# Indirect gathers with an add in the transfer become plain copies added by the vector engine, in a two-layer mixture-of-experts kernel

## The reference, cut to what matters

```python
x = L0_attn_a_x                                  # 8 x 512 x 128, f32
x = x + attn_a(layernorm(x), ...)                # causal, 16 heads, RoPE
x = x + ffn(layernorm(x), sel, keys, values)     # layer 0 of the experts
x = x + attn_b(layernorm(x), WQ, WK, WV)         # band of 64, one head
x = x + ffn(layernorm(x), sel, keys, values)     # layer 1, same weights

def ffn(x, expert_sel, keys, values):            # 64 experts of size 128
    sel = sigmoid(x @ expert_sel.T)
    sel_val, sel_idx = top_k(sel, 4)
    gates = zeros.at[token, sel_idx].set(sel_val)
    return sum_e (relu(x @ keys[e]) * gates[:, e]) @ values[e]
```

## Time and profile before

| what | value |
|---|---|
| three runs | 1194.97, 1205.8 and 1199.96 us, median 1199.96 us |
| span of the profiled execution | 1216.6 us from first to last instruction |
| what lies around the span | no time is given for it |
| POOL busy | 876.4 us, 72% of the span |
| PE busy | 818.3 us, 67% |
| DVE busy | 728.4 us, 60% |
| ACT busy | 560.2 us, 46% |

### The profile page before, as it was taken

One profiled execution on the slowest core, in us unless ns is written; L12 is line 12 of the kernel. 1 busy time (PEld: TensorE's weight loads), 2 busy tenths in 40 slices (PEclk: granted clock), 3 DMA queues, 4 the chain that ended last, 5 costly groups with the idle time before them and its releaser, 6 DMA issues.

```text
span 1216.6 us, 22596 instructions
## 1 busy us (share of the span) xinstructions
PE 818.3 (67%) x7290; PEld 601.3 (49%) x7290; DVE 728.4 (60%) x2057; ACT 560.2 (46%) x1505; POOL 876.4 (72%) x934
## 2 busy tenths in 40 slices
PE   1899978888688766697898665454458874991000
PEld 0444444443344325697898644343357774991000
DVE  3787988888878424764667846566256772661111
ACT  1177666676566743564565413333126552661000
POOL 6345667879767675887888878878727578887776
PEclk9789999999999986898999866567679897996555
DMA  6556544533272332599898412212325564994222
GB/s 182 171 181 210 191 159 172 171 99 105 75 232 58 96 95 76 144 264 215 176 215 177 81 44 42 39 46 37 100 72 162 149 183 127 263 273 106 69 63 63
DMA packets 226258, 163.80 MB, mean 135 GB/s; under 512 B 15968, under 2 KB 213600, under 8 KB 226144
## 3 DMA queue, kind: packets, MB, share of 16 engines
q1 hardware_dynamic: 183968, 110.43, 31.7%
q0 software_dynamic: 36096, 33.59, 13.8%
q10 hardware_dynamic: 6080, 18.35, 4.1%
HBM read 78.94 MB, written 83.36 MB: 133 GB/s over the span
## 4 chain that ended last, share of the span: by engine, by line
PE 37%; POOL 23%; DVE 15%; issue 14%; ACT 6%; another core or an unknown queue 3%; DMA 3%; ACTq 0%; POOLq 0%; DVEq 0%; SPq 0%
POOL x_res L1743 7%; PE ps L771 6%; PE ps L780 5%; PE ps L672 5%; POOL sorted_rows L1727 4%; POOL v_aug L1745 3%; PE ps L631 3%; PE ps L760 3%; POOL x_scaled L1745 2%; ACT arena L978 2%; DMA x_res<-result_rows,dest 2%; DVE row_max L1211 2%; PE ps L689 2%; POOL arena L1776 1%
## 5 line engine op out<-in xcount | busy, mean ns | idle before, releaser
L1743 POOL DMA_INDIRECT x_res<-result_rows,dest x176 | 274.1, 1557 | 60.6 <-issue 48.8
L978 ACT ACTIVATE arena<-ps 128x512 f32<-128x512 f32 x320 | 182.8, 599 | 79.9 <-PE ps L604 75.1
L1727 POOL DMA_INDIRECT sorted_rows<-v_aug,dest x144 | 139.7, 970 | 83.7 <-issue 33.8
L1410 DVE COPY arena<-ps 128x512 f32<-128x512 f32 x128 | 88.2, 689 | 132.0 <-PE ps L760 71.7
L771 PE MATMUL ps<-arena 128*128 128x128 f32 x1024 | 147.2, 290 | 23.0 <-DVE arena L1410 11.5
L631 PE MATMUL ps<-arena 64*128 64x128 bf16 (+3 forms) x576 | 130.2, 305 | 28.9 <-DMA arena<-k_parts 15.1
L771 PEld LDWEIGHTS ps<-arena 128*128 128x128 f32 x1024 | 134.4, 205 | 26.9 <-issue 13.9
L1211 DVE TENSOR_REDUCE row_max<-ps 128x1 f32<-128x512 f32 (+1 forms) x192 | 127.0, 682 | 33.6 <-PE ps L651 31.9
L967 ACT COPY arena<-ps 128x512 f32<-128x512 f32 x128 | 75.0, 586 | 145.6 <-PE ps L780 117.0
L780 PE MATMUL ps<-arena 128*128 x1024 | 140.1, 281 | 0.9 <-ACT arena L967 0.9
L1727 POOL DMA_INDIRECT sorted_rows<-x_scaled,dest x112 | 111.5, 995 | 35.9 <-issue 24.6
(11 more groups left out here) (207 smaller groups left out, 1649.5 us busy)
## 6 DMA issues: line engine op xcount, KB each, us to landing
arena<-sorted_rows SPq DMA_DIRECT2D x128, 256.0 KB
result_rows<-arena SPq DMA_DIRECT2D x128, 256.0 KB
sorted_rows<-arena ACTq DMA_DIRECT2D x16, 1024.0 KB, 4.6
arena<-q_parts SPq DMA_DIRECT2D x16, 512.0 KB, 4.0
arena<-k_parts SPq DMA_DIRECT2D x16, 512.0 KB, 5.0
q_parts<-parts SPq DMA_DIRECT2D x52, 128.0 KB, 2.8
k_parts<-parts SPq DMA_DIRECT2D x38, 128.0 KB, 3.0
x_res<-result_rows,dest POOLq DMA_INDIRECT x176
```

What stands on the lines that cost most here:

```text
L978: nc.scalar.activation(prob[:, grp % 2, pr % 2, PROB_AT[u]:PROB_AT[u] + T], ps[:, v % 2, :], ACT.Exp, scale=SCALE_A).then_inc(exp_done, 1)
L1410: nc.vector.tensor_copy(xtt[:, n % 2, :], ps[:, e_bank(0, layer, half, n), :]).then_inc(t1_done, 1)
L1727: g.indirect_dma_start(sorted_d[b // HALF][:, :], bass.IndirectOffsetOnAxis(dest[:, 16 * b + n:16 * b + n + 1], 0), scaled_rows(layer, b)[ ...
L1743: g.indirect_dma_start(x[:, TT * b + t, :], None, rows, index, compute_op=ALU.add).then_inc(lane, 16)
```

## The change

Three things. **(a)** All 16 batches are gathered by plain copies. Each choice c of a batch goes into a slice of 128x512 of its own (`gathered_slice`), in buffers that are free at that time: in layer 0 two sets in turn (`x_scaled`; and one of `w_attn`, `parts`, `max_t`, `arena`), in layer 1 seven sets. A copy into a slice waits until the add of the slice's last user is done (`slice_freed`). **(b)** DVE adds one slice at a time: layer 0's batch 0 before iteration -1, batch b + 2 at four places of iteration b; layer 1's slices behind every second expert step of the last half from step 8 on, the others after the last step. The gathers of batches 5 to 7 of layer 0 move one iteration ahead in POOL's row. **(c)** The 74 clearings `rest` are gone.

```diff
-PLAIN = tuple((1, b) for b in range(3, B))
-PACED_FROM = 5
+ADD_FROM, ADD_EACH = 8, 2
...
+def gathers_ahead(it):
+    return {-1: (2,), 0: (3,), 1: (4, 5)}.get(it, ())
+def gathers_behind(it):
+    return {2: (6,), 3: (7,)}.get(it, ())
+def added_count(layer, b, c):
+    return TOPK * (B * layer + b) + c + 1
...
-        mt = sb("max_t", [32, 2, T], BF16)
+        max_room = sb("max_t", [P, 2, T], BF16)
+        mt = max_room[0:32, :, :]
...
+        spare = [w[:, 0:T], parts[:, 2].rearrange("p n t -> p (n t)").bitcast(F32),
+                 max_room[:, :, :].rearrange("p n t -> p (n t)").bitcast(F32), arena[:, 9504:9504 + T]]
+        heads = [ytf[:, i, :] for i in range(8)]
+        ropes = [qt[0], qt[1], kt[0], kt[1]]
+        first_homes = (four_slices(xs_a), spare)
+        second_homes = (four_slices(xs_a), four_slices(xs_b[:, 0]), four_slices(xs_b[:, 1]), spare, heads[0:4], heads[4:8], ropes)
...
+        def slice_freed(layer, b, c):
+            if layer == 0:
+                return added_count(0, b - 2, c) if b >= 2 else 0
+            before = {0: (0, B - 2), 3: (0, B - 1), 7: (1, 0)}
+            return added_count(*before[b], c) if b in before else 0
...
-            def add_rows(layer, b):
+            def add_rows(layer, b, c):
-                xb = x[:, TT * b:TT * b + TT, :]
-                for c in range(TOPK):
-                    for lane in landed:
-                        dve.wait_ge(lane, landed_count("gather", layer, b) - 16 * (TOPK - 1 - c))
-                    if c:
-                        dve.wait_ge(added, TOPK * PLAIN.index((layer, b)) + c)
-                    nc.vector.tensor_tensor(xb, xb, gathered_rows(layer, b)[:, TT * c:TT * c + TT, :], ALU.add).then_inc(added, 1)
+                xb = x[:, TT * b:TT * b + TT, :].rearrange("p t n -> p (t n)")
+                for lane in landed:
+                    dve.wait_ge(lane, landed_count("gather", layer, b) - 16 * (TOPK - 1 - c))
+                if c:
+                    dve.wait_ge(added, added_count(layer, b, c - 1))
+                nc.vector.tensor_tensor(xb, xb, gathered_slice(layer, b, c), ALU.add).then_inc(added, 1)
...
+                add_soon(b + 2, 0)
                 beside(b, 5)
...
             for s in range(STEPS):
                 expert_step(1, 1, s)
-            for b in range(B):
-                if (1, b) in PLAIN:
-                    add_rows(1, b)
+                if s >= ADD_FROM and (s - ADD_FROM) % ADD_EACH == 0:
+                    add_rows(1, *soon.pop(0))
+            for b, c in soon:
+                add_rows(1, b, c)
...
-                adding = (layer, b) not in PLAIN
-                if not adding and last_reader(layer, b):
-                    pool.wait_ge(added, last_reader(layer, b))
                 for c in range(TOPK):
+                    if slice_freed(layer, b, c):
+                        pool.wait_ge(added, slice_freed(layer, b, c))
                     for t in range(TT):
...
-                        if adding:
-                            g.indirect_dma_start(x[:, TT * b + t, :], None, rows, index, compute_op=ALU.add).then_inc(lane, 16)
-                        else:
-                            g.indirect_dma_start(gathered_rows(layer, b)[:, TT * c + t, :], None, rows, index).then_inc(lane, 16)
+                        g.indirect_dma_start(gathered_slice(layer, b, c)[:, P * t:P * t + P], None, rows,
+                                             bass.IndirectOffsetOnAxis(dest[:, at:at + 1], 0)).then_inc(lane, 16)
...
                     for n in range(TT * TOPK):
                         scatter(1, late, n)
-                        if late >= PACED_FROM:
-                            rest()
```

More of the change, by code:

```diff
@@ L156, in transfer_order @@
     for b in range(-1, LAST_IT_B + 1):
-        far, late = b + 3, b - 2
-        if b <= 1:
-            out.append(("gather", 0, far))
+        out += [("gather", 0, far) for far in gathers_ahead(b)]
+        late = b - 2
         if 0 <= late < B:
             out.append(("scatter", 1, late))
-        if 1 < b < B - 3:
-            out.append(("gather", 0, far))
+        out += [("gather", 0, far) for far in gathers_behind(b)]
     return out + [("gather", 1, b) for b in range(B)]
@@ L411, in scaled_rows, with four_slices, gathered_slice @@
             return xs_b[:, b % 2] if layer or b == B - 1 else xs_a
-        gather_buffers = (xs_a, xs_b[:, 0], xs_b[:, 1])
-        def gather_buffer(layer, b):
-            return b % 3 if layer else 0
-        def gathered_rows(layer, b):
-            return gather_buffers[gather_buffer(layer, b)]
-        def last_reader(layer, b):
-            mine = PLAIN.index((layer, b))
-            earlier = [n for n in range(mine) if gather_buffer(*PLAIN[n]) == gather_buffer(layer, b)]
-            return TOPK * (earlier[-1] + 1) if earlier else 0
+        def four_slices(rows):
+            return [rows[:, TT * c:TT * c + TT, :].rearrange("p t n -> p (t n)") for c in range(TOPK)]
+        spare = [w[:, 0:T], parts[:, 2].rearrange("p n t -> p (n t)").bitcast(F32),
[4 more added lines that the diff above has]
+        second_homes = (four_slices(xs_a), four_slices(xs_b[:, 0]), four_slices(xs_b[:, 1]), spare, heads[0:4], heads[4:8], ropes)
+        def gathered_slice(layer, b, c):
+            homes = second_homes if layer else first_homes
+            return homes[b % len(homes)][c]
+        def slice_freed(layer, b, c):
[3 more added lines that the diff above has]
+            return added_count(*before[b], c) if b in before else 0
         def scaled_in(it, k):
@@ L575, in _ @@
             for b in range(B):
-                if (1, b) not in PLAIN:
-                    for lane in landed:
-                        sp.wait_ge(lane, landed_count("gather", 1, b))
-                else:
-                    sp.wait_ge(added, TOPK * (PLAIN.index((1, b)) + 1))
+                sp.wait_ge(added, added_count(1, b, TOPK - 1))
                 sp.dma_start(out_d.rearrange("(t p) c -> p t c", p=P)[:, TT * b:TT * b + TT, :],
@@ L1585, in combined_stats @@
             def combined_stats(b):
-                if (0, b) in PLAIN:
-                    add_rows(0, b)
-                    dve.wait_ge(added, TOPK * (PLAIN.index((0, b)) + 1))
-                else:
-                    for lane in landed:
-                        dve.wait_ge(lane, landed_count("gather", 0, b))
+                dve.wait_ge(added, added_count(0, b, TOPK - 1))
                 finish(ln_stats(x[:, TT * b:TT * b + TT, :], st0, mv0, rs0, b, ln2))
@@ L1600, in _ @@
             dve.wait_ge(band_made, BANDS)
+            for c in range(TOPK):
+                add_rows(0, 0, c)
             for b in range(-1, LAST_IT_B + 1):
@@ L1705, in _ @@
             g.tensor_tensor(maskswap, maskswap, upper, ALU.add).then_inc(swapped, 1)
-            transfers, rests = count(), count(1)
-            def rest():
-                n = next(rests)
-                if n > 1:
-                    pool.wait_ge(rested, n - 1)
-                g.memset(w[:, :], 0.0).then_inc(rested, 1)
+            transfers = count()
             def next_lane():
@@ L1835, in _ @@
             gather(0, 0)
+            pool.wait_ge(parts_out, 192 * B)
+            for i in range(2):
+                pool.wait_ge(mrow_out[i], 16 * B)
             gather(0, 1)
             for b in range(-1, LAST_IT_B + 1):
-                far, late = b + 3, b - 2
-                if b <= 1:
+                late = b - 2
+                for far in gathers_ahead(b):
                     gather(0, far)
@@ L1846, in _ @@
                         scatter(1, late, n)
[L1847 to L1849 removed]
+                for far in gathers_behind(b):
                     gather(0, far)
```

15 lines of the change are left out of this document (8 added, 7 removed).

## The result

The changed kernel takes 1123.03 us (median of 4 runs, 1120.06 to 1127.7), the kernel before 1197.93 us beside it (1194.97 to 1205.8): ratio 0.9384, 95% interval 0.9352 to 0.9416, so 75 us (6.2%) faster. Forecast were 35 us and 1165, with a range down to 1135: the direction was right, and the size came out at twice the forecast and outside the range.

What follows compares the result with a forecast made beforehand. Bound by stretches: PE's expert steps, POOL from 696 to 892 us, PE and transfer engines from 1021, POOL alone at the end. Terms -24.3 - 11 + 4 - 7.7 + 4 = -35.0 us from 1199.96 gave 1165 us, range 1135 to 1212.

Steps and rivals of the forecast that it cites:

- part a: Gathers as plain copies: -24.3 us in the last run, -11 us in the middle for two waits, PE's and DVE's.
- What is late next is ACT's copy of the attention input at 864 us: Middle, before layer 1's first step: this copy limits what the two removed waits give, so -11 us was counted.
- The last run, -24.3 us: Layer 1's gathers to the end: 48 adding gathers become copies, -30.3 us, with 6 us back; bounds -30.3 and +17.
- the +6 us for copies held by their landings: Last run: about 59 copies beside expert steps take 1.35 us each, losing 0.10 us apiece.
- R2: Less gain: landings hold copies to 1.55 us, iteration 6 stays late; 1188 us, chance 0.20; sign: landing waits over 15 us.
- The clearings, -7.7 us on the path: Batch 7's 16 scatters before layer 1's gathers: without clearings the last run starts 7.7 us earlier; the 58 others hide.
- The unspaced scatters, +4 us: Scatters that lose their clearings, beside expert steps: may hold up other engines; +4 us, bounds 0 and +70.
- R1: Slower: unspaced transfers hold up other engines at layer 0's end and layer 1's batches 5 and 6; 1216 us, chance 0.15.
- The adds, +4 us: DVE's 64 adds, 20 before: mostly hidden, but one per iteration lengthens the path to the destinations; bounds 0 and +22.
- That the change doesn't do what it says, with DVE standing in iterations for unlanded slices, I give nothing of its own: Iterations of the middle: no chance of its own for DVE waiting on slices, because the slices have 40 us.
- The contention named from the Trainium skill: Last run: 32 two-input DVE adds could block POOL's issues, up to 22 us; not counted in the sum.
- R3: More gain: nameless stretches come from POOL's full row, half of their 46 us goes too; 1142 us, chance 0.13.

Runs made afterwards that it cites:

- a_busy_less: Changed kernel with two or three (2.5 in the mean) small POOL clearings behind each of layer 0's gathers: 1168.7 us, ratio 0.9771.
- run 14: Not a numbered run: in "the last run 14 us" it is the stretch from layer 1's first gather to the end, worth 14 us by a_l1_adding.
- a_l1_adding: Changed kernel with batches 0 to 2 of layer 1 adding in the transfer again and DVE's layer 1 adds behind the last step: 1138.6 us, ratio 0.9504.
- b_no_rest: Kernel before without the 74 clearings, nothing else changed: 1186.37 us, ratio 0.993.
- a_rest: Changed kernel with the 74 clearings back behind the same scatters, plus some waits to keep them off the slices: 1134.33 us, ratio 0.949.
- a_order: Changed kernel with layer 0's gathers of batches 5, 6 and 7 back at their old places: 1141.94 us, ratio 0.9533.
- the two doses: Two runs of the changed kernel with small POOL clearings behind each layer 0 gather: four gave 1214.57 us, 2.5 in the mean 1168.7 us.
- before_again: Kernel before, unchanged, run and profiled again: 1193.78 us, ratio 1.0009, span 1190.9 us.
- a_flight4: Changed kernel with four gathers or scatters in flight in place of three: 1110.52 us, ratio 0.931.
- a_late_adds: Changed kernel with all 32 adds of layer 1 behind the last expert step: 1125.34 us, ratio 0.941.
- b_plain_l1: Kernel before with all eight batches of layer 1 copied and added by DVE behind the last step, three buffers: 1187.96 us, ratio 0.9955.

## Why the prediction was wrong

**Where the 75 us come from.** By undoing one part at a time: POOL's time at layer 0's gathers 46 us (`a_busy_less`), the last run 14 us (`a_l1_adding`), the clearings 8 to 13 us (`b_no_rest`, `a_rest`). Together 68 to 73 of 75, each good to some 5 us; the order is worth 4 us beside them in a full row, and keeping the old one loses 18 of the gain (`a_order`).

**The step that failed** is this one of part a: "In the middle, layer 0's 128 gathers give POOL 128 x 0.61 = 78 us. That is worth only what somebody waited for. Two such places are in the trace", with 13.67 and 1.24 us, and from them -11 us (bounds 0 and -15). The rule is right, the waits were read from a trace in which nameless waits had hidden them. Before DVE's wait at 851 us there are the first two stretches of the earlier trace rows and a third nameless wait of ACT that the prediction did not name (the rows of the kernel before, ACT in order of time):

```profile
821.24 0.38 ACT L1094 ACTIVATE sigmoid<-ps 128x256 f32<-128x256 f32 x1 [9.45 <-remote]
...
864.00 0.59 ACT L1081 COPY xnt<-ps 128x512 f32<-128x512 f32 x1 [7.60 <-remote]
```

10.04 + 19.58 + 9.45 = 39 us, near the 43 by which DVE's wait is shorter in that trace. While ACT, PE and DVE stood, POOL worked on, and so DVE found its rows there: 1.24 us in place of 44.6. (The stretch of 16.28 us, from 878.8 to 895.0, lies behind that wait.) Without them the waits return. The term is 46 us of the 78 (POOL has some 30 us of room instead, by the two doses), and its bounds (0 to -15) lay short of it.

It could have been seen beforehand. POOL's row from the first gather of layer 0 to the last scatter of batch 3 ran from 544.13 to 870.52, where the next batch's scatters begin: 326 us, in which POOL waits less than 10 us in all for anything but its own gaps between transfers. And the prediction itself wrote that POOL "hardly rests" from 696 to 892 us. What was missing was to lay POOL's instructions end to end and ask who would wait if the nameless stretches weren't there. `before_again` bears it out: without them it needs 323 us for the same row (535.3 to 858.4), so the 39 us that the others lost made POOL's row 3 us longer. Also missing was weight on a sign that was in hand: the profiled execution was 16.6 us above the median of the runs, and that was carried along as a constant.

**The step "What is late next is ACT's copy of the attention input at 864 us"** failed with it. That copy stood in a nameless wait of 7.60 us itself (the row above), so its lateness was of that one execution too. In after PE's first step of layer 1 comes at 813.28 us, 48.9 us earlier than in `before_again` (862.17), and still waits 5.58 us.

**The last run, -24.3 us**: measured -14. The mis-sized term is the +6 us for copies held by their landings. The copies beside expert steps took 1.54 us each (48 from 938.2 to 1012.3 us), not 1.35, and POOL's waits for landings there are 12.4 + 4.4 us, the sign that the prediction gave to R2 (over 15). `a_flight4` confirms the cause. Against 1.253 us a copy that is 48 x 0.29 = 14 us, and the other 79, at 1.27 us each, add 1.5: -30.3 + 15.4 = -14.9.

**The clearings, -7.7 us on the path**: measured 7.2 us in the trace and 8.4 in the runs; right. That the other 58 hide is right but for 2 us of batches 5 and 6 in the changed kernel (`a_rest`); layer 0's 26 show nothing beyond what executions differ by.

**The unspaced scatters, +4 us, and R1** (the rival on the slower side): nothing of it. `b_no_rest` is faster, and in after ACT and DVE have no nameless wait of over 2 us in the middle. It rested on the three stretches, which came in no other profile.

**The adds, +4 us**: at most a few us. In after DVE waits 2.1 us for slices in layer 0, at one add, and `a_late_adds` shows that the 13 adds between the last steps are free and not needed there. "That the change doesn't do what it says, with DVE standing in iterations for unlanded slices, I give nothing of its own" was right only because of the new order; with the old one DVE stands over 20 us.

**The contention named from the Trainium skill** ("SBUF — State Buffer", section "Who interferes with whom"), priced at up to 22 us: the prediction took one rule of that section, and left out that the same section reports no stalled DMA from a DVE `tensor_tensor`, which is what these adds are, and infers that issuing a DMA needs the write interface, of which a `tensor_tensor` takes nothing. The trace agrees with that: the copies beside 13 adds take 0.95 us and those beside none (`a_late_adds`) take 0.94 to 0.95. The sum went by the row, and the runs agree with the row.

**R2** (1188 us) had the pace of the last run right (1.55 forecast, 1.54 measured) and the middle wrong. **R3** (1142 us) named the full row of POOL, but as the cause of the stretches. It isn't: `before_again` has the full row and no stretches. The row's fullness cost time by itself.

## What to carry to other kernels

A wait that is short in one trace is no proof of slack: if anything in that trace held the waiting engine back (a wait without a name, an execution longer than the usual ones), lay the busiest engine's instructions end to end through the stretch and compare with the time it took; where the two agree, that engine is the pace, and each microsecond taken from it counts nearly in full until the next limit (here 46 of 78). The accumulation inside an issued transfer was paid on the issuing engine here, at 0.6 us a transfer; a vector engine with idle time did it cheaper, given buffers enough to keep the issuer from waiting for the adds (`b_plain_l1` hadn't them). Order paid only once the engine had room.

## What the runs showed that was not expected

The adding form of the indirect transfer has no price that could be seen here (within 1 us in one pair of traces, within some 9 us in the whole times) apart from its issue time on POOL: copies with 2.5 small clearings each (79 us on POOL's row) take the same 358 us for the same row of transfers as adding transfers do, although the adding form keeps the transfer engines busy for 0.50 of it in place of 0.39. A POOL clearing of 128x128 takes 0.21 us in a chain, so with its gap it can be used as a dose of POOL's time in steps of about 0.25 us. And a window of three transfers, enough where landings take 2.54 us (the last one in after), costs some 9 us in 74 where the expert steps' traffic is beside them; a fourth in flight takes most of it back.
